# Turning the scan result of a decoder kernel with 32x32 block transposes on VectorE and sixteen small DMAs in place of eight TensorE transposes

## The chip, the cores and the metric

The kernel runs on one core of one Trainium2 chip. The metric is the device time of one execution in microseconds (us), lower is better. A core has TensorE (matrix products, results into PSUM; PE in the profile, its weight loads PEld), VectorE (DVE), ScalarE (ACT), GpSimd (POOL) and the queues that issue transfers; here almost all transfers are issued by SyncE (SP). The engines run their own instruction lists in order and meet at semaphores.

## The reference, cut to what matters

One decoder layer over 16 batches of 256 rows by 512 channels. The middle of its three parts is the one that the change touches: a decaying sum over the rows of the squared context, channel by channel (key and value are both the context), whose result multiplies the row x.

```python
def _L0_xattn_ref(q, k, v, decay):
    kv = kh * vh                      # k and v are both ctx
    def step(r, inc):
        r = d * r + inc               # a decay for each of 16 heads
        return (r, r)
    _, rs = jax.lax.scan(step, r0, kv_t)
    out = qh * jnp.moveaxis(rs, 0, 1)

x = _layernorm(x + attention(x))                       # 1
x = _layernorm(x + _L0_xattn_ref(x, ctx, ctx, decay))  # 2
x = _layernorm(x + ffn(x))                             # 3, a quantised FFN 512 -> 2048 -> 512
```

So the second sum is x * (1 + rs): each row of x times one plus its scan state.

## The kernel before

**Tiles.** A batch is 256 rows; row tiles put 128 rows on the partitions (two of them, q = 0 and 1, in `rows`), while the attention products and the scan put channels on the partitions (four tiles of 128 channels by 256 rows, `xT_in`, `ctx_sb`). The scan runs along the free dimension, so its result stands channels by rows in `ctx_sb` and has to be turned to rows by channels before it can meet `rows`.

**The software pipeline.** Each engine's list is written out by hand: a `lead`, then `body(j)` for j = 1 to 15 (called turn j here), then a `drain`. Turn j works on attention of batch j, on the projection, the first two layernorms and the first FFN product (`f`) of batch j-1, on the inner normalisation of the FFN of batch j-2, and on the second FFN product (`y`) and the last layernorm of batch j-3. What an engine does in a turn stands in one fixed order, so a wait at one place holds all that stands behind it on that engine.

**The path of the scan.** ScalarE squares the context in `ctx_sb` (`ctx_square`). VectorE, at the very end of its turn, runs four scans and one clip in place (`scan`, L1003 and L1006). In the next turn TensorE turns the result with eight 128x128 transposes into two PSUM banks (`r`, `r_product`, L1455), between `shiftT(j, 2)` and `shifted(j, 2)`. VectorE then forms x * (1 + state) in `layernorm2_sum` (L1029), once for each row tile, as one `scalar_tensor_tensor` whose first operand is the PSUM bank and whose second is `rows`:

```python
dv.scalar_tensor_tensor(rows_of(b)[:, q, :], bank_of("r", q, b), SCAN_SCALE, rows_of(b)[:, q, :],
                        ALU.add, ALU.mult).then_inc(S["ln2"], 1)
```

`statistics` follows each (L1013, L1015). After both, GpSimd makes the inverse deviation (`inverse_std2`), ScalarE normalises, VectorE quantises (`quantise_x`, which also fills `x_round`), ScalarE stores `xq`, SP turns it with a DMA transpose (`transpose_x`, xqT<-xq), and TensorE multiplies (`f`, L1467).

**What stands around it.** On VectorE the order in a turn is: `layernorm3_sum(j-3, 0)` (L1130), `layernorm1_sum(j-1, 0)`, `maxima(j, 1)` (L962), ..., `z_add(j-2, 0)` (L1085), `maxima(j, 2)`, `attn_norm`, `qk_lo(j, 3)`, `layernorm3_sum(j-3, 1)` (L1130), the two `layernorm2_sum(j-1, .)`, `z_max`, `maxima(j, 3)`, ..., `z_add(j-2, 1)`, `quantise_x(j-1)`, ..., `scan(j)`. On GpSimd, `attn_split(j, 1)` (L437, L440) is followed at once by `g_mul(j-2, 1)` (L547), a product of two SBUF tiles of 128x2048 elements. On TensorE, `y(j, 1)` (L1474) stands before `shiftT(j, 2)`; `shiftT(j, 3)` (L1367) waits for `maxima(j, 3)`, and all of the rest of TensorE's turn stands behind it. On SP a turn is `load_xT(j+1)`, `transpose_z(j-3, 1)` (hqT<-h, which `y(j, 1)` needs), `store_out`, `load_ctx(j)`, `transpose_x(j-1)`, `store_out`, `transpose_z(j-2, 0)`, `load_rows(j)`.

**PSUM banks.** Banks 6 and 7 go round between `y`, `o`, `r`, `v` and `f`; `take` makes the next user wait until the reader of the one before is done.

Of the kernel before, what the change touches and what calls it, by code (L numbers as in the profile page):

```python
# [12 lines left out]
ALU = mybir.AluOpType  # L13
AX_X = mybir.AxisListType.X

P = 128
# [27 lines left out]
NROW = NPART * NPART  # L44
NROWS = 3


def decoder_kernel(nc, x, xT, ctxT, W, L, bq, bk, bv, bo, decay, w1T, b1, ln_g, ln_b, w2T, b2, out):
    b1_scratch = nc.dram_tensor("b1_scratch", (NPART, INNER), BF16, kind="Internal").ap()

    with ExitStack() as ctx:
# [68 lines left out]
        def sem(name):  # L120
# [39 lines left out]
            (PE, "shifted_ready", 4), (PE, "scores_ready", 4), (PE, "qk_ready", 4), (PE, "v_ready", 2),  # L160
            (PE, "shiftT_ready", 4), (PE, "pv_ready", 4), (PE, "o_ready", 2), (PE, "rT_ready", 2),
            (PE, "f_ready", 8), (PE, "y_ready", 2),
# [7 lines left out]
            (DV, "qk_lo", 8), (DV, "max_done", 4), (DV, "shift_split", 8), (DV, "inverted", 12), (DV, "attn_done", 4),  # L170
            (DV, "scan_done", 5), (DV, "ln1", 6), (DV, "ln2", 6), (DV, "x_quant", 14),
            (DV, "z_added", 4), (DV, "z_quant", 12),
# [6 lines left out]
            (SP, "xT_loaded", 16), (SP, "x_loaded", 16), (SP, "ctx_loaded", 16), (SP, "out_stored", 32),  # L179
            (SP, "xqT_loaded", 16), (SP, "hqT_loaded", 64),  # L180
        ]
        per = {n: k for _, n, k in table}
# [19 lines left out]
        def half_rows(b, q):  # L202

            t = h_of(b, q)[:, :].bitcast(BF16)
            return t.rearrange("p (i k) -> p i k", i=2)[:, :, 0:INNER // 2]

        def rows_of(b):
            return rows[b % NROWS]

        users = [("y", 0, 3, "ln3", 1), ("o", 0, 1, "ln1", 1), ("o", 1, 1, "ln1", 4), ("y", 1, 3, "ln3", 4),  # L210
                 ("r", 0, 1, "ln2", 1), ("r", 1, 1, "ln2", 4), ("v", 0, -1, "v_stored", 1),
                 ("v", 1, -1, "v_stored", 2)]
        users += [("f", u, 1, "silu_done", u + 1) for u in range(8)]
# [3 lines left out]
        LAST, PRIOR, THIRD = NB - 1, NB - 2, NB - 3  # L217
        drain_bank = {("o", LAST, 0): 7, ("o", LAST, 1): 6, ("r", LAST, 0): 2, ("r", LAST, 1): 3,
                      ("y", THIRD, 0): 0, ("y", THIRD, 1): 1, ("y", PRIOR, 0): 4, ("y", PRIOR, 1): 5,
# [6 lines left out]
        def drain_hqT(b, q):  # L226

            if b == PRIOR and q == 0:
                return hqT[:, :, :]
            if b == LAST and q == 1:  # L230
                t = v_sb[PRIOR % 2][:, :, :].rearrange("p q d -> p (q d)").bitcast(BF16)
            else:
                t = probs[:, LAST - b if b == PRIOR else 0, :, :].rearrange("p i t -> p (i t)").bitcast(BF16)
            return t.rearrange("p (k t) -> p k t", t=P)

        def fz_of(b):
# [16 lines left out]
        def ffw(n):  # L253
            return h[FFW_BUFFER[n]][:, :]

        def flat(t):
            return t.rearrange("p a b -> p (a b)")

# [13 lines left out]
        def _(sp):  # L272
# [33 lines left out]
            def load_ctx(b):  # L306
                wait(sp, "rT_ready", b - 1, 2)
                if b == 0:
                    sp.wait_ge(u_merge, 5)
                sp.dma_start(ctx_sb[:, :, :], ctxT[b]).then_inc(S["ctx_loaded"], 16)  # L310

            def load_rows(b):
# [43 lines left out]
            def body(j):  # L356
                if alive(j, -1):
                    load_xT(j + 1)
                if alive(j, 3):
                    transpose_z(j - 3, 1)  # L360
                    store_out(j - 3, 0)
                load_ctx(j)
                transpose_x(j - 1)
                if alive(j, 3):
                    store_out(j - 3, 1)
                if alive(j, 2):
                    transpose_z(j - 2, 0)
                load_rows(j)
# [14 lines left out]

            def drain():
                transpose_z(THIRD, 1)
                transpose_x(LAST)
                store_out(THIRD, 0)
                store_out(THIRD, 1)
                transpose_z(PRIOR, 0)
                drain_transpose(PRIOR, 1)  # L390
                drain_transpose(LAST, 0)
                drain_transpose(LAST, 1)
                store_out(PRIOR, 0)
                store_out(PRIOR, 1)
                store_out(LAST, 0)
                store_out(LAST, 1)
# [546 lines left out]
        def _(dv):  # L943
# [53 lines left out]
            def scan(b):  # L997

                wait(dv, "ctx_squared", b, 1)
                if b == 0:  # L1000
                    dv.wait_ge(u_decay, 16 * GH)
                for c in range(KC):
                    dv.tensor_tensor_scan(ctx_sb[:, c, :], decay_col[:, c:c + 1].to_broadcast([P, T]),  # L1003
                                          ctx_sb[:, c, :], 0.0, ALU.mult, ALU.add).then_inc(S["scan_done"], 1)
                wait(dv, "scan_done", b, KC)
                dv.tensor_scalar(flat(ctx_sb[:, :, :]), flat(ctx_sb[:, :, :]), STATE_MAX, -STATE_MAX, ALU.min,  # L1006
                                 ALU.max).then_inc(S["scan_done"], 1)

            def statistics(ln, b, q, k, tile_rows):
# [15 lines left out]
            def layernorm2_sum(b, q):  # L1025

                wait(dv, "rT_ready", b, q + 1)
                wait(dv, "norm1", b, q + 1)
                dv.scalar_tensor_tensor(rows_of(b)[:, q, :], bank_of("r", q, b), SCAN_SCALE, rows_of(b)[:, q, :],  # L1029
                                        ALU.add, ALU.mult).then_inc(S["ln2"], 1)  # L1030
                statistics(2, b, q, 3 * q + 1, rows_of(b)[:, q, :])
# [281 lines left out]
        def _(pe):  # L1313
# [134 lines left out]

            def r(j, q):

                r_product(take(j, "r", q, "scan_done", j - 1, 5), q)

            def r_product(p, q):
                for kc in range(KC):
                    last = pe.transpose(p[:, kc * P:(kc + 1) * P], ctx_sb[:, kc, q * P:(q + 1) * P], ident[:, :])  # L1455
                last.then_inc(S["rT_ready"], 1)

            def f(j, u):
# [43 lines left out]
            def drain():  # L1502
# [3 lines left out]
                wait(pe, "probs_ready", LAST, 8)  # L1506
                wait(pe, "scan_done", LAST, 5)
                for q in range(NT):
                    r_product(bank_of("r", q, LAST), q)
                drain_y(THIRD, 0)  # L1510
# [7 lines left out]
                drain_f(5, "ln3", THIRD, 4)  # L1518
                drain_f(6, "ln2", LAST, 1)
                drain_f(7, "ln2", LAST, 4)  # L1520
                for at, (b, q) in enumerate(((PRIOR, 0), (PRIOR, 1), (LAST, 0), (LAST, 1))):
# [69 lines left out]
            def body(j):  # L1591
# [29 lines left out]
                if alive(j, 0):  # L1621
                    shiftT(j, 2)
                if alive(j, 1):
                    r(j, 0)
                    if j == 1:
                        pe.wait_ge(u_scale, 5)
                    r(j, 1)

                if alive(j, 0):
                    shifted(j, 2)  # L1630
# [11 lines left out]
                if alive(j, 0):  # L1642
                    shifted(j, 3)
                if alive(j, -1):
                    v(j, 1)
# [68 lines left out]
```

## Time and profile before

| | |
|---|---|
| median of 3 runs | 1051.52 us (1050.95 to 1052.96) |
| the profiled execution's own time | 1050.39 us |
| its span, first to last instruction | 1048.6 us |
| TensorE | 950.2 us busy, 91% of the span |
| VectorE | 891.9 us, 85% |
| ScalarE | 827.4 us, 79% |
| GpSimd | 605.4 us, 58% |
| the chain that ended last | 60% on TensorE, 26% on VectorE, 6% on transfers |
| mean granted TensorE clock | 0.962 of full speed |

A share of busy time is an average over lead, 15 turns and drain, and a TensorE that is shown busy is not one at its peak. What bounds a turn is read from the chain of waits within one turn and from the instructions that had to wait. Turns 3 to 14 repeat within a few tenths of a microsecond every 58 us; times below are from the span's start, and the rows shown of one turn are those of turn 7, from about 436 to 494 us.

### The profile page before, as it was taken

The page shows a single profiled execution, that of the slowest core. Times are in us where ns is not written, and L with a number is a line of the kernel's source. Part 1 is how long each engine was busy: PE and PEld are TensorE (multiplying, and loading weights), DVE is VectorE, ACT ScalarE, POOL GpSimd, SP SyncE. Part 2 cuts the span into 40 slices and gives each one's busy share as a digit, 9 for nine tenths or more (in the row PEclk, how much of TensorE's full clock was granted, in tenths as well). Part 3 has the DMA queues.
Part 4 walks back from the last instruction along what each step waited for, and adds up shares of the span by engine and source line. Part 5 has one row for each costly group of instructions (what it writes and reads, how often), then busy time and mean ns, then how long its engine had stood idle before and what let it go on. Part 6 is the DMA issues. An engine that isn't in the chain of part 4 may idle for free.

```text
span 1048.6 us, 23525 instructions
## 1 busy us (share of the span) xinstructions
PE 950.2 (91%) x9388; PEld 655.1 (62%) x9388; DVE 891.9 (85%) x1474; ACT 827.4 (79%) x957; POOL 605.4 (58%) x767
## 2 busy tenths in 40 slices
PE   5998997999999999999999999999999999978416
PEld 3766756676767767676767767676767677644102
DVE  4577868989898999989898989899898989995766
ACT  3646686888979797988888797978889797977684
POOL 2332337474766749485757658494757566572653
PEclk9999998999999999999999999999999999988668
DMA  9432200213122121323131121323231321122213
GB/s 357 158 111 113 72 3 21 74 52 84 23 71 61 43 76 52 84 52 83 35 100 23 56 68 44 83 52 84 52 84 21 79 56 54 42 52 63 53 30 91
DMA packets 106352, 73.68 MB, mean 70 GB/s; under 512 B 91386, under 2 KB 91386, under 8 KB 104451
## 3 DMA queue, kind: packets, MB, share of 16 engines
q1 hardware_dynamic: 105522, 70.34, 24.2%
q8 instruction: 75, 1.23, 0.5%
q10 hardware_dynamic: 720, 1.84, 0.5%
q14 instruction: 35, 0.28, 0.1%
HBM read 41.73 MB, written 8.40 MB: 48 GB/s over the span
## 4 chain that ended last, share of the span: by engine, by line
PE 60%; DVE 26%; DMA 6%; ACT 4%; issue 3%; POOL 1%; SPq 0%; POOLq 0%; DVEq 0%; ACTq 0%
PE bank L1333 21%; PE bank L1467 11%; PE bank L1474 9%; DMA xqT<-xq 5%; PE wave L1382 4%; PE bank L1396 4%; PE wave L1358 3%; DVE neg_max L962 3%; DVE h L1085 3%; PE bank L1400 3%; DVE stats L1013 3%; PE bank L1468 3%; DVE fz L1090 2%; DVE rows L1029 2%; DVE qx L1052 1%
## 5 line engine op out<-in xcount | busy, mean ns | idle before, releaser
L962 DVE TENSOR_REDUCE neg_max<-wave 128x8 f32<-128x2048 f32 x64 | 146.2, 2284 | 39.0 <-PE wave L1358 39.0
L547 POOL TENSOR_TENSOR h<-h,g_tile 128x2048 f32<-128x2048 f32 x30 | 139.9, 4663 | 39.1 <-ACT h L738 39.1
L655 ACT ACTIVATE probs<-wave 128x1024 f32<-128x1024 f32 x128 | 124.4, 1024 | 40.5 <-PE wave L1382 40.3
L1467 PE MATMUL bank<-w,xqT 128*128 128x512 fp8e4 x496 | 129.7, 384 | 20.6 <-DMA xqT<-xq 20.6
L437 POOL TENSOR_SCALAR attn_hi<-attn 128x256 fp32r<-128x256 f32 x64 | 31.8, 497 | 150.1 <-DVE attn L995 134.8
L717 ACT ACTIVATE h<-bank,qx 128x512 f32<-128x512 f32 x124 | 83.8, 689 | 24.4 <-PE bank L1468 22.1
L693 ACT ACTIVATE rows<-rows,rstd 128x512 f32<-128x512 f32 x96 | 74.3, 807 | 33.1 <-POOL rstd L453 18.5
L1085 DVE TENSOR_TENSOR h<-h,b_tile 128x2048 f32<-128x2048 f32 x32 | 84.0, 2624 | 17.0 <-POOL h L547 16.9
L1467 PEld LDWEIGHTS bank<-w,xqT 128*128 128x128 bf16 x496 | 47.8, 99 | 78.0 <-issue 17.4
L1474 PE MATMUL bank<-w,hqT 128*128 128x512 fp8e4 x416 | 94.3, 380 | 0.0
L496 POOL TENSOR_TENSOR rows<-rows,bo_tile 128x512 f32<-128x512 f32 x32 | 52.6, 1665 | 71.2 <-DMA rows<-x 71.2
L1003 DVE TENSOR_TENSOR_SCAN ctx_sb<-decay_col,ctx_sb 128x256 f32<-128x256 f32 x64 | 78.8, 1290 | 0.0
L1333 PE MATMUL bank<-xT_hi,wq_hi 128*128 128x256 f32 x256 | 78.4, 306 | 0.1
L440 POOL TENSOR_TENSOR attn_lo<-attn,attn_hi 128x256 fp32r<-128x256 f32 x64 | 73.7, 1151 | 5.3
L1382 PE MATMUL wave<-qk_parts 32*128 32x256 f32 x1536 | 73.4, 301 | 3.6 <-ACT shift_rows L677 3.6
L670 ACT ACTIVATE qk_parts<-bank,bias_qk 128x256 fp32r<-128x256 f32 x128 | 53.6, 474 | 25.9 <-PE bank L1333 25.9
L1396 PE MATMUL bank<-probs,v_sb 128*32 128x256 f32 x1024 | 70.6, 394 | 3.1 <-ACT probs L655 2.1
L1333 PE MATMUL bank<-xT_lo,wq_hi 128*128 128x256 f32 x256 | 73.3, 286 | 0.0
L1333 PE MATMUL bank<-xT_hi,wq_lo 128*128 128x256 f32 x256 | 73.2, 286 | 0.0
L738 ACT ACTIVATE h<-h,fs 128x2048 f32<-128x2048 f32 x32 | 66.8, 2089 | 7.8 <-POOL fs L538 7.8
L1358 PE MATMUL wave<-qk_parts 32*128 32x256 f32 x1536 | 63.7, 296 | 10.1 <-ACT probs L655 8.0
L1382 PEld LDWEIGHTS wave<-qk_parts 32*128 32x128 f32 x1536 | 56.9, 190 | 25.0 <-issue 20.1
(181 smaller groups left out, 2844.1 us busy)
## 6 DMA issues: line engine op xcount, KB each, us to landing
ctx_sb<-ctxT SPq DMA_DIRECT2D x16, 512.0 KB, 3.8
rows<-x SPq DMA_DIRECT2D x16, 512.0 KB, 4.0
out<-rows SPq DMA_DIRECT2D x32, 256.0 KB, 2.5
xT_in<-xT SPq DMA_DIRECT2D x15, 512.0 KB, 4.7
h<-w1T SPq DMA_DIRECT2D x4, 1024.0 KB, 14.6
h<-w2T SPq DMA_DIRECT2D x4, 1024.0 KB, 4.8
h<-Wq SPq DMA_DIRECT2D x1, 1024.0 KB, 6.2
h<-Wk SPq DMA_DIRECT2D x1, 1024.0 KB, 9.8
```

Of the source, the lines that this page charges most:

```text
L547: po.tensor_tensor(h_of(b, q)[:, :], h_of(b, q)[:, :], g_tile[:, :], ALU.mult).then_inc(done, 1)
L655: ac.activation(probs[:, kt, :, :], wave[:, :, kt * T:(kt + 1) * T], ACT.Exp, scale=SM_SCALE).then_inc(S["probs_ready"], 1)
L717: ac.activation(h_of(b, q)[:, n * FW:(n + 1) * FW], bank_of("f", u, b), ACT.Silu, scale=qx[:, X_DEQ, q:q + 1]).then_inc(S["silu_done"], 1)
L962: dv.tensor_reduce(neg_max[:, :, :], wave[:, :, :].rearrange("p j (t k) -> p j t k", t=NT), axis=AX_X, op=ALU.max, negate=True).then_inc(S ...
L1003: dv.tensor_tensor_scan(ctx_sb[:, c, :], decay_col[:, c:c + 1].to_broadcast([P, T]), ctx_sb[:, c, :], 0.0, ALU.mult, ALU.add).then_inc(S[" ...
L1085: dv.tensor_tensor(h_of(b, q)[:, :], h_of(b, q)[:, :], b_tile[:, :], ALU.add).then_inc(S["z_added"], 1)
L1333: last = pe.matmul(psum, lhsT, rhs, start=(first and i == 0), stop=(final and i == len(pairs) - 1))
L1358: last = pe.matmul(bank[head][:, qt * T:(qt + 1) * T], parts[at, qp, qt * P:(qt + 1) * P], parts[at, kp, :], start=(i == 0), stop=(i == 2))
L1382: last = pe.matmul(bank[head][:, kt * T:(kt + 1) * T], keys, queries, start=(i == 0), stop=(i == 3))
L1396: pe.matmul(bank[4][i * HD:(i + 1) * HD, 0:T], v_sb[b % 2][:, kt, ch:ch + HD], probs[:, kt, i, :], start=(kt == 0), stop=(kt == NT - 1))
L1467: pe.matmul(p[:, :], xqT[:, q, kc, :], w1[:, kc, n * FW:(n + 1) * FW], start=(kc == 0), stop=False)
L1474: last = pe.matmul(p[:, :], hqT[:, k, :], w2[:, k, :], start=(k == 0), stop=(k == FC - 1))
```

## The change

The state is no longer turned by TensorE. At the end of `scan`, VectorE writes the clipped state with two `transpose` instructions (each 128 partitions by 512 elements, every 32x32 block turned in itself) into `x_round`. SP then moves the blocks to their places with sixteen DMAs (`move_state`), each 32 partitions by 256 elements in pieces of 32 elements (128 bytes), from `x_round` back into `ctx_sb`, which now holds rows by channels. `layernorm2_sum` reads the state from `ctx_sb` in SBUF where it read a PSUM bank. `load_ctx` of the next batch waits for the second `layernorm2_sum`, where it waited for TensorE's transposes. The eight transposes are gone from TensorE's turn, from its drain and from the round of banks. SP's new `move_state(j-1)` stands right behind `load_xT(j+1)`, and first in SP's drain.

```diff
+SB = P // HD
...
-            (PE, "shiftT_ready", 4), (PE, "pv_ready", 4), (PE, "o_ready", 2), (PE, "rT_ready", 2),
+            (PE, "shiftT_ready", 4), (PE, "pv_ready", 4), (PE, "o_ready", 2),
...
-            (DV, "scan_done", 5), (DV, "ln1", 6), (DV, "ln2", 6), (DV, "x_quant", 14),
+            (DV, "scan_done", 7), (DV, "ln1", 6), (DV, "ln2", 6), (DV, "x_quant", 14),
...
+            (SP, "state_moved", 16 * SB * SB),
...
-                 ("r", 0, 1, "ln2", 1), ("r", 1, 1, "ln2", 4), ("v", 0, -1, "v_stored", 1),
-                 ("v", 1, -1, "v_stored", 2)]
+                 ("v", 0, -1, "v_stored", 1), ("v", 1, -1, "v_stored", 2)]
...
+        state_blocks = flat(x_round[:, :, :])
+        state_rows = flat(ctx_sb[:, :, :])
...
             def load_ctx(b):
-                wait(sp, "rT_ready", b - 1, 2)
+                wait(sp, "ln2", b - 1, 4)
...
+            def move_state(b):
+
+                wait(sp, "scan_done", b, 7)
+                for a in range(SB):
+                    for s in range(SB):
+                        to = state_rows[s * HD:(s + 1) * HD, :].rearrange("p (n a c) -> p n a c", a=SB, c=HD)
+                        block = state_blocks[a * HD:(a + 1) * HD, s * T:(s + 1) * T]
+                        sp.dma_start(to[:, :, a, :],
+                                     block.rearrange("p (n c) -> p n c", c=HD)).then_inc(S["state_moved"], 16)
...
                 if alive(j, -1):
                     load_xT(j + 1)
+                move_state(j - 1)
...
             def drain():
+                move_state(LAST)
                 transpose_z(THIRD, 1)
...
+                wait(dv, "scan_done", b, KC + 1)
+                wait(dv, "xq_stored", b - 1, 1)
+                blocks = state_blocks.rearrange("p (s q k c) -> p q k s c", s=SB, q=NT, c=HD)
+                for q in range(NT):
+                    dv.transpose(blocks[:, q, :, :, :],
+                                 ctx_sb[:, :, q * P:(q + 1) * P].rearrange("p k (s c) -> p k s c", c=HD)
+                                 ).then_inc(S["scan_done"], 1)
...
-                wait(dv, "rT_ready", b, q + 1)
+                wait(dv, "state_moved", b, 16 * SB * SB)
                 wait(dv, "norm1", b, q + 1)
-                dv.scalar_tensor_tensor(rows_of(b)[:, q, :], bank_of("r", q, b), SCAN_SCALE, rows_of(b)[:, q, :],
-                                        ALU.add, ALU.mult).then_inc(S["ln2"], 1)
+                dv.scalar_tensor_tensor(rows_of(b)[:, q, :], state_rows[:, q * D:(q + 1) * D], SCAN_SCALE,
+                                        rows_of(b)[:, q, :], ALU.add, ALU.mult).then_inc(S["ln2"], 1)
...
-            def r(j, q):
-
-                r_product(take(j, "r", q, "scan_done", j - 1, 5), q)
-
-            def r_product(p, q):
-                for kc in range(KC):
-                    last = pe.transpose(p[:, kc * P:(kc + 1) * P], ctx_sb[:, kc, q * P:(q + 1) * P], ident[:, :])
-                last.then_inc(S["rT_ready"], 1)
...
-                wait(pe, "scan_done", LAST, 5)
-                for q in range(NT):
-                    r_product(bank_of("r", q, LAST), q)
...
-                drain_f(6, "ln2", LAST, 1)
-                drain_f(7, "ln2", LAST, 4)
+                drain_f(6, "probs_ready", LAST, 8)
+                drain_f(7, "probs_ready", LAST, 8)
...
                 if alive(j, 0):
                     shiftT(j, 2)
-                if alive(j, 1):
-                    r(j, 0)
-                    if j == 1:
-                        pe.wait_ge(u_scale, 5)
-                    r(j, 1)
-
-                if alive(j, 0):
                     shifted(j, 2)
```

## Rows read from the trace of the kernel before

**Rows 1.** The chain of waits in turn 7: start, length (us), what.
```profile
458.59 3.57 PE bank L1474 x16
...
462.19 0.76 DVE rows L1130
...
480.97 3.38 DMA xqT<-xq
```

**Rows 2.** Timeline of TensorE, turn 7: start, length, instruction, [idle before, what ended it].
```profile
472.06 0.38 PE L1367 MATMUL wave<-ident,shift 128*128 128x128 f32 x2
...
484.49 1.02 PE L1467 MATMUL bank<-w,xqT 128*128 128x512 fp8e4 x4 [0.72 <-DMA xqT<-xq]
```

**Rows 3.** Timeline of VectorE, turn 7.
```profile
441.68 0.70 DVE L1006 TENSOR_SCALAR ctx_sb<-ctx_sb 128x1024 f32<-128x1024 f32 x1
...
446.65 2.29 DVE L962 TENSOR_REDUCE neg_max<-wave 128x8 f32<-128x2048 f32 x1 [1.14 <-PE wave L1358]
...
454.66 2.48 DVE L1085 TENSOR_TENSOR h<-h,b_tile 128x2048 f32<-128x2048 f32 x1 [1.34 <-POOL h L547]
...
463.81 0.68 DVE L1029 SCALAR_TENSOR_TENSOR rows<-bank,rows 128x512 f32<-128x512 f32 x1
...
465.35 0.68 DVE L1029 SCALAR_TENSOR_TENSOR rows<-bank,rows 128x512 f32<-128x512 f32 x1
```

**Rows 4.** Timeline of GpSimd, turn 7.
```profile
463.36 0.73 POOL L440 TENSOR_TENSOR attn_lo<-attn,attn_hi 128x256 fp32r<-128x256 f32 x1
464.05 4.66 POOL L547 TENSOR_TENSOR h<-h,g_tile 128x2048 f32<-128x2048 f32 x1
```

**Rows 5.** All instructions of two lines: ns shortest/median/longest, first and last start.
```profile
L1029 DVE SCALAR_TENSOR_TENSOR rows<-bank,rows x30: 678/679/682, 108.9 to 930.3; 128x512 f32<-128x512 f32 x30
...
L986 DVE STREAM_TRANSPOSE sums_T<-bank x64: 432/443/450, 46.6 to 946.9; 128x256 f32<-128x256 f32 x64
```

**Rows 6.** Timelines of VectorE and GpSimd, one place in the drain and one in turn 6.
```profile
987.92 6.49 DVE L1085 TENSOR_TENSOR h<-h,b_tile 128x2048 f32<-128x2048 f32 x1
...
987.45 4.80 POOL L547 TENSOR_TENSOR h<-h,g_tile 128x2048 f32<-128x2048 f32 x1 [4.84 <-ACT h L738]
...
434.16 1.99 DVE L1117 TENSOR_SCALAR h<-h,fz 128x2048 f32<-128x2048 f32 x1
...
433.80 3.48 POOL L496 TENSOR_TENSOR rows<-rows,bo_tile 128x512 f32<-128x512 f32 x2 [4.92 <-DMA rows<-x]
```

**Rows 7.** SP's timeline; DMA issues with KB and us to landing; the queue's packets, MB, share.
```profile
430.49 0.49 SPq L304 DMA_DIRECT2D xT_in<-xT  x1
452.59 2.62 SPq L334 DMA_TRANSPOSE hqT<-h  x2
...
2.14 0.83 SPq L279 DMA_DIRECT2D bv_col<-bv  x1
...
35.00 1.29 SPq L343 DMA_DIRECT2D b_scratch<-b_parts  x3
...
b_scratch<-b_parts SPq DMA_DIRECT2D x3, 4.0 KB, 2.4
...
hqT<-h SPq DMA_TRANSPOSE x58, 3.2
...
q1 hardware_dynamic: 105522, 70.34, 24.2%
```

**Rows 8.** Windows: length, busy time and instructions by engine, granted clock, DMA, GB/s.
```profile
930.00:937.30 7.30, 3.28 (x58) 1.94 (x58) 7.09 (x11) 5.22 (x7) 6.48 (x13) 1.00 0.29 94
937.30:950.90 13.60, 8.36 (x71) 4.36 (x72) 12.72 (x30) 10.44 (x11) 5.75 (x9) 0.50 0.23 53
...
90.80:94.20 3.40, 3.40 (x30) 1.66 (x23) 2.87 (x6) 2.90 (x6) 0.00 (x0) 0.50 0.62 255
```

**Rows 9.** The chain of waits at the transposes of turn 1 and of the drain.
```profile
107.97 1.70 PE bank L1455 x8
...
964.92 0.87 PE wave L1455 x8
```

More of the change, by code:

```diff
@@ L205, in half_rows, with flat @@
             return t.rearrange("p (i k) -> p i k", i=2)[:, :, 0:INNER // 2]
+        def flat(t):
+            return t.rearrange("p a b -> p (a b)")
         def rows_of(b):
@@ L217, in decoder_kernel @@
         LAST, PRIOR, THIRD = NB - 1, NB - 2, NB - 3
-        drain_bank = {("o", LAST, 0): 7, ("o", LAST, 1): 6, ("r", LAST, 0): 2, ("r", LAST, 1): 3,
+        drain_bank = {("o", LAST, 0): 7, ("o", LAST, 1): 6,
                       ("y", THIRD, 0): 0, ("y", THIRD, 1): 1, ("y", PRIOR, 0): 4, ("y", PRIOR, 1): 5,
@@ L254, in ffw @@
             return h[FFW_BUFFER[n]][:, :]
-        def flat(t):
-            return t.rearrange("p a b -> p (a b)")
         def merge_bank(m, kc):
@@ L1643, in body @@
                     shifted(j, 3)
+                if j == 1:
+                    pe.wait_ge(u_scale, 5)
                 if alive(j, -1):
```

## The prediction

> **What bounds the kernel now.** The page's chain first: it lies 60% on TensorE and 26% on VectorE (table above), so neither alone sets the time. Within one turn, the chain of waits shows how they share it [rows 1]: TensorE's y(j, 1) ends at 462.16; VectorE's layernorm3_sum starts at 462.19 and the chain stays on VectorE, gap after gap of some 0.02 us, through both layernorm2_sum and quantise_x to 480.9; the transpose xqT takes 3.38; then TensorE's f starts at 484.49. From there to the next y(j, 1) it is TensorE without a break. So a turn of 58 us is a TensorE stretch (f to y, some 36 us) and a VectorE stretch (18.8 us) with a transfer behind it. In the VectorE stretch TensorE has other work, and runs out of it 0.72 before f [rows 2]. In the TensorE stretch VectorE has spare time: it waits 1.14 for scores and 1.34 for GpSimd's g_mul [rows 3]. Work taken from TensorE pays only in its own stretch, and work put on VectorE costs in full only in its own.
>
> **Part by part.** The sum is made against the profiled execution, 1050.39 us.
>
> *The transposes leave TensorE.* Eight took 0.87 in the drain and 1.70 in turn 1, on the chain both times [rows 9]: -2.6 us. In the other turns they stand just behind y(j, 1), in the VectorE stretch, where TensorE waits for xqT at the end anyway [rows 2]: 0.
>
> *Two block transposes on VectorE.* A block transpose of 256 elements a partition takes 0.443 [rows 5]. For 512 I bound it by 0.44 (all overhead) and 0.89 (all length), and take 0.71, one element a cycle beyond a fixed part, like other 512-element VectorE rows here (0.68) [rows 3]: two make 1.45 with their gaps. They stand behind the clip that ends at 442.38. VectorE then reaches maxima(j, 1) at about 447.0 in place of 445.5, where it had waited until 446.65: 0.35 late, and z_add's wait of 1.34 swallows that [rows 3]. GpSimd's small deviation steps behind layernorm3_sum come 1.45 later too, and I leave 0.1 a turn for their way to g_mul (0 to 0.5 by the bounds).
>
> *Sixteen DMAs.* SP has nothing to issue between 431.0 and 452.59 [rows 7], so move_state starts at 443.9. One issue takes 0.43 in a row of three (1.29) and 0.83 at the dearest [rows 7]; the new ones have 256 pieces each, and I take 0.5, nearer to the run of three. Sixteen end at about 451.9; a small transfer lands 2.4 after its issue [rows 7]: state at 454, wanted at 463.81. Data: the queue's 105522 packets took 24.2% of 16 engines' span, 38 ns each [rows 7]; 4096 new ones at that price are 9.9 us of all sixteen engines, which still ends near 454, and these packets are smaller than the mean. Behind move_state on SP stands transpose_z(j-3, 1), now issued at 452.59: two issues, the second landing 3.2 later, about 457.1, for y(j, 1) at 458.59 [rows 1, 7]. So the transfers cost 0 so long as an issue stays under some 0.63; at 0.83 y would be 3.8 late. load_ctx moves about 5 us back and has until the end of the turn.
>
> *layernorm2_sum reads SBUF.* Here I see the price. With a PSUM operand L1029 takes 678 to 682 ns in all thirty rows [rows 5], though GpSimd's g_mul (L547, two SBUF inputs) runs beside it: L440 is busy from 463.36 to 464.09 and g_mul from 464.05 to 468.71, while the two L1029 stand at 463.81 and 465.35 and aren't touched [rows 3, 4]. Where both engines read two SBUF tensors they don't overlap: z_add in the drain took 6.49, starting 0.47 behind a g_mul of 4.80 [rows 6], against 2.48 in turn 7 [rows 3]; 4.33 of waiting and 2.16 of work, so VectorE stood until g_mul was through. Who goes first is seen in turn 6: GpSimd issued two L496 in a row, 433.80 to 437.28, and VectorE's L1117, issued at 434.16, ended at 436.15, in the middle of the pair [rows 6]. So the instruction already waiting goes before GpSimd's next.
>
> The Trainium skill says the same ("SBUF — State Buffer", Who interferes with whom): a VectorE instruction with two SBUF inputs contends with a GpSimd instruction that reads SBUF, as an exclusive lock, and the later one stands still until the other ends. The trace agrees, with the 6.49 above. L1029's own rows, which never moved, would price this edit at 0; the rule prices it at what is left of a g_mul.
>
> For turn 7: the first L1029 issues at 463.81, waits for L440 until 464.09, runs 0.6: 464.7, 0.2 late. g_mul goes next, about 464.65 to 469.3. The second L1029, wanted at 465.6, waits until 469.3 and ends at 469.9, against 466.03: 3.8 late, all of it in the VectorE stretch. Were g_mul to go first, the first L1029 would wait until 468.71: 4.8. Over the turns g_mul starts 0.19 to 0.27 behind the first L1029 in twelve (3 to 14) and 0.86 ahead of it in turn 15 (3.6 late there); in turn 2 VectorE then waits long for TensorE anyway; turn 1 has no g_mul. So 13 turns pay 3.8, with 4.8 as the upper bound.
>
> *What this does to TensorE.* shiftT(j, 3) waits for maxima(j, 3), and slides from 472.06 [rows 2] to 475.9; TensorE, rid of the transposes, runs dry about 471.7: some 4 us idle. In turn 15 it was busy for 3.28 of 7.30 us, and the granted clock then fell to 0.50 (1.2 GHz) for 13.6 us; in the lead it fell for 3.4 [rows 8]. A fall of 3.4 costs 1.7 of TensorE's work, of which 11.7 us lie between shiftT and f's place (484.49 less the 0.72): f at 475.9 + 11.7 + 1.7 = 489.3, against 488.3 for a late xqT alone. I take 0.7 a turn; bounds 0 (no fall) and 10.9 (all 11.7 at 1.2 GHz), and go by the shorter fall, since no second idle place of such length follows.
>
> **Sum.** 13 x (3.8 + 0.1 + 0.7) = 59.8; less 2.6: +57.2, so 1107.6 for the profiled execution, and 1108.7 from the median, which lies 1.1 above it. I say 1108.
>
> **The rivals.** *Not slower: the lock doesn't hold for this instruction.* scalar_tensor_tensor with an immediate might be let through where the plain sum of rows 6 wasn't. Then 13 x 0.1 - 2.6 = -1.3: 1049.1 for the profiled execution, 1050.2 from the median, 0.13% under before. It decides if a wait of the second L1029 stays under 0.2 us. Against it: both of its inputs come from SBUF, like z_add's.
>
> *The transfers are late.* If an issue costs 0.83, y(j, 1) is 3.8 late; its layernorm2_sum then meets a g_mul already running, so that the two delays overlap to about 4.8 a turn: 13 x (4.8 + 0.1 + 0.7) - 2.6 = +70, 1121. If the sixteen went one after the other at 2.4 us each, the state would land at 443.9 + 38.4 = 482.3, 18.5 late: 13 x 18.5 - 2.6 = +238, 1288. For it: sixteen small transfers in one queue. Against: three issues took 1.29 together and each landed after 2.4 [rows 7], so they overlap.
>
> The Trainium skill ("DMA: Bandwidth & Descriptors", Rules for kernel authors) wants small transfers coalesced, since under 64 KB one pays mostly overhead; these are 32 KB each. By its fixed 2 us each, in a row, I estimate a state 12 us late and a time near 1204; no row here shows transfers that wait for one another like that.
>
> *The block transposes are dear.* At three times their length (4.3 us) 2.8 us a turn would pass the slack of VectorE's TensorE stretch: +36 on top, 1144. The 0.443 of rows 5 hardly moves over 64 instances, so I give this little.
>
> **Chances.** Lock as worked out: 0.76, with a range of its own from 1087 (3.0 a turn in all) to 1131 (4.8, the 0.1 and 1.5 for the clock). Late transfers 0.10, of which 0.03 one after the other; half of the 0.10 above 1140. Not slower 0.10. Dear block transposes and the rest 0.04. The range 1080 to 1140 leaves out 0.18. About 0.2% (2.1 us) is what a measurement of this kernel tells from no change: slower 0.88, same 0.07 and faster 0.05, the last two from the second case, whose sum lies close to that bound.
>
> **What would show it.** Of the new profile: L1029's successor with one of its two instances at 4 us or more in turns 3 to 15, next to an L547 that ends just before it does (right), or at 0.7 (wrong); turns of 62 to 63 us; VectorE's transposes at 0.7; sixteen issues in some 8 us; state landing before VectorE asks for it; TensorE idle before shiftT(j, 3), and a granted clock under 1.00 in those turns, where it was 1.00 before. Wrong would be: VectorE waiting for state_moved, y waiting for hqT, or an L1029 that isn't held.

## The result, and the profile after

| | before | after |
|---|---|---|
| median | 1051.73 us (1050.95 to 1052.96, 4 runs) | 1123.58 us (1121.18 to 1125.73, 4 runs) |
| ratio | 1 | 1.0674 (95% interval 1.0652 to 1.0696) |
| profiled execution, its span | 1050.39, 1048.6 us | 1125.73, 1123.9 us |

Slower by 71 us (by the ratio), against the 57 forecast; 1123.6 lies within the range of 1080 to 1140. A kernel's time, below, is the median of its runs in the faster of the chip's two states. Below are the lines of the profile after that answer to those of before. First, the page's chain that ended last:

```profile
DVE 34%; PE 31%; SPq 15%; DMA 7%; issue 6%; ACT 5%; POOL 1%; ACTq 0%; POOLq 0%; DVEq 0%
SPq L323 13%; PE bank L1356 11%; DVE ctx_sb L1019 6%; DMA hqT<-h 5%; DVE rows L1052 5%; PE bank L1481 5%; PE bank L1488 4%; DVE neg_max L978 3%; PE wave L1405 3%; DVE stats L1036 3%; DVE h L1140 2%; DVE fz L1113 2%; SPq L348 2%; PE wave L1381 2%; PE bank L1419 2%
```

Where TensorE held 60% before, SP's issuing of the sixteen transfers (L323) now holds 13% by itself. Second, three groups of VectorE over the whole execution (count, busy us, mean ns, idle time before them and what ended it):

```profile
L1052 DVE SCALAR_TENSOR_TENSOR rows<-ctx_sb,rows 128x512 f32<-128x512 f32 x32 | 59.6, 1864 | 4.7 <-DMA ctx_sb<-x_round 4.7
L1028 DVE STREAM_TRANSPOSE x_round<-ctx_sb 128x512 f32<-128x512 f32 x32 | 20.9, 690 | 0.5
L1153 DVE SCALAR_TENSOR_TENSOR rows<-bank,fz,rows 128x512 f32<-128x512 f32 x28 | 20.4, 730 | 24.1 <-PE bank L1488 24.1
```

And layernorm3_sum in the kernel before:

```profile
L1130 DVE SCALAR_TENSOR_TENSOR rows<-bank,fz,rows 128x512 f32<-128x512 f32 x28 | 20.9, 747 | 2.0 <-PE bank L1474 1.2
```

layernorm2_sum (L1052) was L1029 with 679 ns in every instance [rows 5]; at 1864 it holds VectorE for 59.6 - 32 x 0.679 = 37.9 us more. And layernorm3_sum (L1153) waits 24.1 us for y, where it waited 1.2. The two make 61 us; the spans of the two profiled executions lie 75 us apart. The 4.7 us in front of L1052 are one wait, in the drain, for the state to land: behind the last layernorm2_sum of turn 15, the kernel after takes 2.5 us longer to its end. Third, the chain of waits in one turn (start, length, what), the successor of [rows 1], and GpSimd's timeline at the same place:

```profile
531.51 0.68 DVE x_round L1028
...
532.21 0.63 SPq L323
...
536.15 1.26 SPq L323
...
542.68 0.61 SPq L323
...
543.40 1.27 SPq L348
...
544.71 3.19 DMA hqT<-h
...
548.03 3.63 PE bank L1488 x16
...
551.68 0.76 DVE rows L1153
...
553.29 4.41 DVE rows L1052
...
558.55 0.69 DVE rows L1052
...
565.01 0.69 PE wave L1390 x2
```

```profile
551.84 0.73 POOL L456 TENSOR_TENSOR attn_lo<-attn,attn_hi 128x256 fp32r<-128x256 f32 x1
552.52 4.62 POOL L563 TENSOR_TENSOR h<-h,g_tile 128x2048 f32<-128x2048 f32 x1
```

The chain now runs through the change: the second block transpose ends at 532.2, SP issues sixteen transfers until 543.3, and only then hqT (L348), which y(j, 1) needs. y ends at 551.7, so late that g_mul (L563) starts 0.77 ahead of layernorm2_sum; the first L1052 stands until g_mul is through at 557.14 and ends at 557.7. In the kernel before, y came first and g_mul second. Over the turns this varies: the first L1052 took 2.6 to 5.1 us in 11 of the 13 turns from the third on, and 1.1 in two, where g_mul was nearly done. A turn takes 59 to 67 us, 63.6 in the mean, against 58.1. Last, windows of that turn (length, busy us of PE, PEld, DVE, ACT, POOL, granted clock, DMA, GB/s):

```profile
560.00:565.00 5.00, 0.97 (x5) 0.44 (x3) 4.93 (x6) 1.52 (x2) 4.00 (x12) 0.80 0.30 105
565.00:568.40 3.40, 3.38 (x12) 2.35 (x16) 3.30 (x7) 0.42 (x2) 2.08 (x5) 0.50 0.00 0
568.40:571.80 3.40, 3.40 (x40) 2.94 (x41) 3.23 (x7) 2.19 (x3) 2.08 (x2) 0.79 0.00 0
```

TensorE was busy for 0.97 of 5.00 us, and the granted clock fell to 0.50 (1.2 GHz). With 0.50 and 1.00 as its only levels, the means of the three rows make 2.0, 3.4 and 1.4 us at 0.50, 6.8 in all. Over the turns from 176 to 930 us it was 0.96, where it was 1.00 before.

So two things were to be told apart: the lock at layernorm2_sum, which the prediction made its main term, and sixteen issues in front of hqT, which it had put at 0.

### The profile page after: what moved, and what is told of

It is laid out like the page before. It is cut to its first block, busy times and chain, and to the rows that moved or that the text cites. A ratio compares the mean times of both kernels' runs of the same rounds, so it can differ in the third digit from the quotient of the medians.

```text
span 1123.9 us, 23542 instructions
## 1 busy us (share of the span) xinstructions
PE 961.0 (86%) x9260; PEld 655.7 (58%) x9260; DVE 943.9 (84%) x1506; ACT 829.0 (74%) x957; POOL 606.3 (54%) x767
## 3 DMA queue, kind: packets, MB, share of 16 engines
q10 hardware_dynamic: 720, 1.84, 0.5%
## 4 chain that ended last, share of the span: by engine, by line
DVE 34%; PE 31%; SPq 15%; DMA 7%; issue 6%; ACT 5%; POOL 1%; ACTq 0%; POOLq 0%; DVEq 0%
SPq L323 13%; PE bank L1356 11%; DVE ctx_sb L1019 6%; DMA hqT<-h 5%; DVE rows L1052 5%; PE bank L1481 5%; PE bank L1488 4%; DVE neg_max L978 3%; PE wave L1405 3%; DVE stats L1036 3%; DVE h L1140 2%; DVE fz L1113 2%; SPq L348 2%; PE wave L1381 2%; PE bank L1419 2%
## 5 line engine op out<-in xcount | busy, mean ns | idle before, releaser
L563 POOL TENSOR_TENSOR h<-h,g_tile 128x2048 f32<-128x2048 f32 x30 | 139.3, 4645 | 38.8 <-ACT h L754 38.8
L453 POOL TENSOR_SCALAR attn_hi<-attn 128x256 fp32r<-128x256 f32 x64 | 56.3, 879 | 170.1 <-DVE attn L1011 154.8
L1488 PE MATMUL bank<-w,hqT 128*128 128x512 fp8e4 x416 | 97.5, 389 | 19.1 <-DMA hqT<-h 19.1
L1405 PE MATMUL wave<-qk_parts 32*128 32x256 f32 x1536 | 80.9, 321 | 13.5 <-ACT shift_rows L693 13.5
L512 POOL TENSOR_TENSOR rows<-rows,bo_tile 128x512 f32<-128x512 f32 x32 | 48.0, 1522 | 81.4 <-DMA rows<-x 81.4
L1405 PEld LDWEIGHTS wave<-qk_parts 32*128 32x128 f32 x1536 | 63.2, 209 | 38.8 <-issue 20.6
L1488 PEld LDWEIGHTS bank<-w,hqT 128*128 128x128 bf16 x416 | 39.5, 99 | 72.3 <-issue 29.7
L995 DVE SCALAR_TENSOR_TENSOR qk_parts<-bank,bias_qk,qk_parts 128x256 fp32r<-128x256 f32 x128 | 55.6, 476 | 27.7 <-ACT qk_parts L686 27.7
L1019 DVE TENSOR_TENSOR_SCAN ctx_sb<-decay_col,ctx_sb 128x256 f32<-128x256 f32 x64 | 74.6, 1224 | 0.0
```

Of the source, the lines that this page charges most:

```text
L563: po.tensor_tensor(h_of(b, q)[:, :], h_of(b, q)[:, :], g_tile[:, :], ALU.mult).then_inc(done, 1)
L1405: last = pe.matmul(bank[head][:, kt * T:(kt + 1) * T], keys, queries, start=(i == 0), stop=(i == 3))
L1488: last = pe.matmul(p[:, :], hqT[:, k, :], w2[:, k, :], start=(k == 0), stop=(k == FC - 1))
```

## The experiments

My first theory for the profile after was that the late transfers set the turn and hide most of the lock; it came from one of the two turns in which layernorm2_sum waits only 0.4 us. The first four runs were made to test it against the prediction's lock.

**sbuf_read: the lock alone.** In the kernel before, only the operand:

```diff
-dv.scalar_tensor_tensor(rows_of(b)[:, q, :], bank_of("r", q, b), SCAN_SCALE, rows_of(b)[:, q, :],
+dv.scalar_tensor_tensor(rows_of(b)[:, q, :], flat(ctx_sb[:, :, :])[:, q * D:(q + 1) * D], SCAN_SCALE,
+                        rows_of(b)[:, q, :],
```

> The kernel before, in which layernorm2_sum takes its first operand from ctx_sb in SBUF as it stands, channels by rows and not turned (so its output is another one); TensorE's transposes still run and nobody reads them, and load_ctx waits for the second layernorm2_sum. No transfers and no block transposes are added. Theory 'lock' (the prediction's main term): the second layernorm2_sum waits some 3.8 us for g_mul in turns 3 to 15, with a lower clock behind it; 1095 to 1112 us. Rival 'late transfers alone' (the change's +72 us come from the sixteen issues, and the SBUF read costs nothing): layernorm2_sum keeps its 0.68 us in both instances; 1050 to 1053 us.

Measured: 1105.53 us, ratio 1.0497 (1.046 to 1.0533), +52 us. Its timelines of VectorE and GpSimd in one turn:

```profile
542.65 0.75 DVE L1130 SCALAR_TENSOR_TENSOR rows<-bank,fz,rows 128x512 f32<-128x512 f32 x1
...
544.26 0.82 DVE L1029 SCALAR_TENSOR_TENSOR rows<-ctx_sb,rows 128x512 f32<-128x512 f32 x1
...
545.95 4.18 DVE L1029 SCALAR_TENSOR_TENSOR rows<-ctx_sb,rows 128x512 f32<-128x512 f32 x1
```

```profile
544.49 5.09 POOL L547 TENSOR_TENSOR h<-h,g_tile 128x2048 f32<-128x2048 f32 x1
```

This is the prediction's turn: the first L1029 0.14 longer, g_mul next, the second L1029 held from 545.95 until 0.55 behind g_mul's end at 549.58. Counted from the start of layernorm3_sum, the second ends 3.64 us later than in the kernel before (7.48 for 3.84; predicted were 3.8). The same instruction with one operand moved from PSUM to SBUF, and no work added, goes from 0.68 to 4.18 us. The later start of load_ctx isn't the cause: no engine waits for that load in either trace. TensorE's idle place and the clock behind it are there too (windows of the same turn):

```profile
552.00:556.00 4.00, 0.77 (x4) 0.29 (x4) 3.93 (x5) 1.52 (x2) 3.25 (x12) 0.83 0.22 89
556.00:559.40 3.40, 3.40 (x12) 2.37 (x16) 3.30 (x7) 0.53 (x2) 2.14 (x4) 0.50 0.00 0
559.40:562.80 3.40, 3.40 (x39) 2.91 (x36) 3.23 (x8) 2.03 (x3) 1.97 (x2) 0.70 0.02 5
```

**gain_later, scan_early, both_moved: one cause taken away by another order.** In the kernel after:

```diff
+inverse_std2(j - 1)
 g_mul(j - 2, 1)
-inverse_std2(j - 1)
 x_rms(j - 1)
...
+scan(j)
 z_max(j - 2, 1)
 qk_lo(j + 1, 1)
 quantise_z(j - 2, 1)
-scan(j)
```

The upper half is gain_later (GpSimd), the lower scan_early (VectorE); both_moved has both.

> The kernel after, with GpSimd's inverse_std2(j-1) moved ahead of g_mul(j-2, 1), so that g_mul can't stand in front of either layernorm2_sum. The transfers stay as late as they were. Theory 'late transfers' (they set the turn, and the lock lies hidden behind them): the small remainder of the lock goes, 0.4 us in 13 turns, 1115 to 1121 us. Rival 'lock': the 3.8 to 4.6 us a turn come back, 1060 to 1075 us.

> The kernel after, with VectorE's scan(j) (with its clip and block transposes) moved ahead of z_max(j-2, 1), some 8 us earlier, so that the sixteen issues are over before SP has to issue hqT for y(j, 1). Theory 'late transfers over a hidden lock': y(j, 1) is no longer late, and the lock that it hid comes out at the second layernorm2_sum, 3.8 to 4.6 us in 13 turns less the 2.6 us of the transposes, 1095 to 1109 us. Rival 'late transfers alone': 1047 to 1052 us. Rival 'neither': 1120 to 1126 us.

> The kernel after with both moves: scan(j) ahead of z_max(j-2, 1), and inverse_std2(j-1) ahead of g_mul(j-2, 1). If late transfers and lock are the whole of the loss, either enough by itself for most of it: 1047 to 1052 us, with turns of 58 us. If something else that the change brought costs as well (the block transposes on VectorE, the packets of the transfers, the lost order of the PSUM banks), the time stays above 1056 us.

Measured: 1114.22 (1.0585, 1.0546 to 1.0624), 1113.12 (1.0575, 1.0536 to 1.0614) and 1093.23 us (1.0389, 1.037 to 1.0408). The first came out 0.8 us under the band of my theory, and for another reason: the lock had moved. The second lies in none of its three bands. The third stays above 1056 us, where it was expected if something else costs as well. This group is maxima's tiny sum of two SBUF tensors (128x8 elements), in gain_later and in the kernel after, both over the whole execution:

```profile
L986 DVE TENSOR_TENSOR shift<-neg_max,zeros 128x8 fp32r<-128x8 f32 x64 | 45.8, 716 | 2.2
```

```profile
L985 DVE TENSOR_TENSOR shift<-neg_max,zeros 128x8 fp32r<-128x8 f32 x64 | 15.3, 239 | 2.2
```

layernorm2_sum is down to 682 ns, but g_mul, now later, meets L986, which loses 45.8 - 15.3 = 30.5 us. In scan_early the new order has a price of its own: quantise_z(j-2, 1) now stands behind the scan, so the source of hqT is late whatever SP does (chain of waits, in front of y):

```profile
472.45 2.00 ACT h L724
474.45 0.02 issue
474.47 1.27 SPq L348
475.74 0.04 issue
475.78 4.86 DMA hqT<-h
```

both_moved has both of these prices (L986 at 709 ns). So none of the three is a clean test, and the next four change no order on VectorE or GpSimd, or say where they do.

**psum_read: the late transfers alone.** The kernel after, with a PSUM operand and TensorE's transposes again:

```diff
+    last = pe.transpose(p[:, kc * P:(kc + 1) * P], x_round[:, q, kc * P:(kc + 1) * P], ident[:, :])
...
     wait(dv, "state_moved", b, 16 * SB * SB)
-    dv.scalar_tensor_tensor(rows_of(b)[:, q, :], state_rows[:, q * D:(q + 1) * D], SCAN_SCALE,
+    dv.scalar_tensor_tensor(rows_of(b)[:, q, :], bank_of("r", q, b), SCAN_SCALE,
```

> The kernel after with the sixteen transfers and the block transposes kept, but with TensorE's eight transposes back (now of x_round, so the state used is another one and the output too), and layernorm2_sum reading their PSUM bank as in the kernel before; it still waits until the state has landed in ctx_sb, where nobody reads it. So the transfers are as late as in the kernel after, and no lock is possible at layernorm2_sum. Theory 'late transfers hide the lock': only the hidden remainder goes, 0.4 us a turn, less 2.6 us that the transposes bring back: 1115 to 1124 us. Rival 'the lock is the larger part': 1065 to 1080 us.

Measured: 1077.36 us, 1.0234 (1.0212 to 1.0257). This fells "late transfers hide the lock": without the lock 46 of the 71 us are gone, as the rival had it. It is also dearer than the prediction's 0 for the transfers. SP's timeline of one turn:

```profile
451.79 11.27 SPq L324 DMA_DIRECT2D ctx_sb<-x_round  x16
463.16 2.65 SPq L349 DMA_TRANSPOSE hqT<-h  x2
```

**split_moves: the kernel after, without the late hqT.**

```diff
-move_state(j - 1)
+move_state(j - 1, range(SB // 2))
 if alive(j, 3):
     transpose_z(j - 3, 1)
+move_state(j - 1, range(SB // 2, SB))
+if alive(j, 3):
     store_out(j - 3, 0)
```

> The kernel after, with SP issuing eight of the sixteen transfers before hqT (transpose_z(j-3, 1)) and eight behind it, and nothing else moved. hqT can then be issued when its source is ready, some 5 us before y(j, 1) wants it, and the state lands near the time at which layernorm2_sum asks. Theory 'late transfers hide the lock': y is on time and the lock comes out as in the kernel before with an SBUF operand (1105.5 us measured), less the 2.6 us of the transposes: 1096 to 1107 us, one of the two layernorm2_sum at some 4.2 us. Rival 'late transfers alone': 1048 to 1053 us. Rival 'the transfers cost by their data or their number, not by where SP issues them': 1118 to 1125 us.

Measured: 1116.03 us, 1.0598 (1.057 to 1.0625); its second layernorm2_sum takes 4.16 to 4.19 us in eleven turns, as in sbuf_read. With the lock in place, late transfers are worth only 0.76% or 8 us; the band of the theory was missed by 9 us, of which more below.

**psum_split: neither.** psum_read with the order of split_moves.

> As psum_read (layernorm2_sum reads a PSUM bank, TensorE's transposes are back and turn x_round, so the output is another one; 1077.4 us measured), with SP issuing eight of the sixteen transfers ahead of hqT and eight behind it. Theory 'the transfers cost by standing in front of hqT in SP's queue' (the issues took 0.61 us each and 0.05 between them in the traces, 10.5 us for sixteen, and one in a turn took over 1.1): y(j, 1) no longer waits for hqT, and what is left is the dead time of the block transposes, measured at 1.4 us: 1053 to 1058 us. Rival 'they cost by their packets or their number': 1072 to 1079 us. Between the two: the state lands late for layernorm2_sum instead.

Measured: 1054.78 us, 1.0021 (1.0008 to 1.0034). All sixteen transfers, both block transposes and all packets are in it, and 22.4 us (1.0234 less 1.0021) are gone by where SP issues eight of them. layernorm3_sum's wait for y, first in psum_read, then in psum_split:

```profile
L1155 DVE SCALAR_TENSOR_TENSOR rows<-bank,fz,rows 128x512 f32<-128x512 f32 x28 | 20.5, 731 | 27.1 <-PE bank L1499 27.1
```

```profile
L1157 DVE SCALAR_TENSOR_TENSOR rows<-bank,fz,rows 128x512 f32<-128x512 f32 x28 | 20.4, 730 | 0.6 <-PE bank L1501 0.2
```

**blocks_only: the block transposes alone**, as dead work at the end of scan in the kernel before:

```diff
+for q in range(NT):
+    dv.transpose(blocks[:, q, :, :, :],
+                 ctx_sb[:, :, q * P:(q + 1) * P].rearrange("p k (s c) -> p k s c", c=HD)
+                 ).then_inc(S["scan_done"], 1)
```

> The kernel before with the two block transposes of the kernel after added at the end of scan; they write x_round and nobody reads it before it is written anew, so they are dead work of 1.45 us a turn on VectorE. Theory of the prediction (VectorE's waits behind them swallow all but 0.1 us a turn): 1052 to 1055 us. Rival (what was left in the gated kernel, 0.9 us a turn, is theirs: they delay the next turn's layernorm3_sum, GpSimd's deviation behind it, and g_mul and z_add behind that): 1059 to 1066 us.

Measured: 1054.51 us, 1.0028 (1.0008 to 1.0048): 1 to 5 us, the prediction's 1.3 at the lower end. What paid for them is VectorE's wait for scores; the waits of before and of blocks_only over twelve to thirteen turns (total us, times, longest):

```profile
DVE neg_max L962 <- PE wave L1358: 17.4, 14, 4.0
```

```profile
DVE neg_max L966 <- PE wave L1369: 4.1, 2, 3.9
```

**split_gated: the change with both causes taken out.** split_moves, and GpSimd waits until VectorE is past:

```diff
 if alive(j, 2):
+    wait(po, "ln2", j - 1, 4)
     g_mul(j - 2, 1)
```

> As split_moves, and GpSimd's g_mul(j-2, 1) also waits until the second layernorm2_sum(j-1) is through; it then falls into the 5.3 us in which VectorE's next instructions (statistics, z_max, maxima) read one SBUF tensor or PSUM. If late transfers and lock are the whole of the loss, both are gone: 1047 to 1054 us, turns of 58 us, both layernorm2_sum at 0.7 us. If a further cost came with the change (block transposes, packets, clock), it stays: above 1058 us.

Measured: 1065.24 us, 1.0123 (1.0106 to 1.0139). In the turns both causes are gone, and 58 of the 71 us with them; the band was missed by 11 us. Of the 14.5 us between the two profiled spans, 4.0 lie behind turn 15's first layernorm2_sum and 0.9 in each of the twelve turns before it. In the drain all sixteen transfers still go ahead of hqT, and layernorm2_sum waits for the state:

```profile
L1055 DVE SCALAR_TENSOR_TENSOR rows<-ctx_sb,rows 128x512 f32<-128x512 f32 x32 | 24.7, 772 | 5.9 <-DMA ctx_sb<-x_round 5.9
```

In the turns the gate has a price: inverse_std2 stands behind g_mul, so ScalarE's second normalisation is late. That wait before and in split_gated:

```profile
ACT rows L693 <- POOL rstd L472: 6.0, 12, 0.6
```

```profile
ACT rows L712 <- POOL rstd L490: 36.5, 12, 3.1
```

ScalarE's shift_rows stands behind it, and TensorE's scores wait for that (before, then split_gated):

```profile
L1382 PE MATMUL wave<-qk_parts 32*128 32x256 f32 x1536 | 73.4, 301 | 3.6 <-ACT shift_rows L677 3.6
```

```profile
L1408 PE MATMUL wave<-qk_parts 32*128 32x256 f32 x1536 | 72.7, 299 | 36.1 <-ACT shift_rows L696 36.1
```

For xqT TensorE hardly waits any more (1.7 us over the turns, where it was 8.4), so the price runs through the scores and not through quantise_x. That it is the whole of the 0.9 a turn is argued; the block transposes are in this kernel too.

**swap_sums and swap_blocks: tries at a version that beats both kernels.** In both, layernorm2_sum goes ahead of y's reader; in the second the block transposes move too:

```diff
+layernorm2_sum(j - 1, 0)
+layernorm2_sum(j - 1, 1)
 layernorm3_sum(j - 3, 1)
-layernorm2_sum(j - 1, 0)
-layernorm2_sum(j - 1, 1)
...
 layernorm1_sum(j - 1, 0)
+turn_blocks(j - 1)        # swap_blocks: the two transposes, no longer in scan
```

> The kernel after, with SP issuing twelve transfers ahead of hqT and four behind it, and with VectorE's two layernorm2_sum(j-1) ahead of layernorm3_sum(j-3, 1), so that they no longer stand behind y(j, 1) and meet attn_split's short product (0.73 us) in place of g_mul. Theory 'lock at g_mul plus late transfers': both are nearly gone, what is left is a wait of some 0.4 us at L440 and the block transposes: 1049 to 1058 us if those cost 0.1 us a turn, 1058 to 1066 us if they cost 0.9. Rival 'the SBUF operand costs wherever it stands': above 1090 us.

> As swap_sums, with the block transposes moved from the end of scan into the next turn, behind layernorm1_sum(j-1, 0), where VectorE had 1.14 us of waiting for scores; eight transfers go ahead of hqT and eight behind it. If the block transposes cost by delaying layernorm3_sum(j-3, 0) and GpSimd behind it, that goes: 3 to 12 us faster than swap_sums, 1047 to 1054 us. If they cost nothing there, the same time as swap_sums.

Measured: 1069.72 (1.0172, 1.0154 to 1.0191) and 1100.80 us (1.046, 1.0415 to 1.0505). swap_sums has layernorm2_sum at 1113 ns over 176 to 930 us, so most of the lock is gone, yet it misses both of its bands; VectorE is then almost without a pause (its wait for scores is 4.8 us over 176 to 930, where it was 17.4). swap_blocks is a plain miss: the two transposes now start 3.1 us behind the end of the clip, the sixteen transfers come as much later, eight of them behind hqT where swap_sums has four, and layernorm2_sum waited for the state and then met g_mul (VectorE's timeline). The two kernels differ in more than the place of the transposes, so they don't price it.

```profile
478.17 0.69 DVE L1057 SCALAR_TENSOR_TENSOR rows<-ctx_sb,rows 128x512 f32<-128x512 f32 x1 [1.22 <-DMA ctx_sb<-x_round]
...
479.72 4.88 DVE L1057 SCALAR_TENSOR_TENSOR rows<-ctx_sb,rows 128x512 f32<-128x512 f32 x1
```

**before_zmax: is the VectorE stretch what bounds the kernel before?**

```diff
-z_max(j - 2, 0)           # behind layernorm2_sum(j - 1, 1)
...
 quantise_x(j - 1)
+z_max(j - 2, 0)
 quantise_z(j - 2, 0)
```

> The kernel before, with z_max(j-2, 0) (2.25 us on VectorE) moved from behind layernorm2_sum to behind quantise_x(j-1), and the waits' counts adapted; the change under study isn't in it. Theory of the prediction, that a turn is a VectorE stretch from y(j, 1) to xqT and a TensorE stretch from f to y(j, 1): the first becomes 2.25 us shorter, TensorE's wait of 0.72 us for xqT goes in some 13 turns, and the rest is TensorE's own work: 1040 to 1046 us. Rival 'VectorE's order there is slack': 1050 to 1053 us.

Measured: 1075.61 us, 1.0221 (1.0202 to 1.024): slower, outside of both bands. The first stretch got only 0.3 us shorter and not 2.25: maxima(j, 3) (L962) then waits for TensorE's scores (VectorE's timeline of one turn, moved and before):

```profile
472.87 0.75 DVE L1130 SCALAR_TENSOR_TENSOR rows<-bank,fz,rows 128x512 f32<-128x512 f32 x1 [0.19 <-PE bank L1473]
...
479.46 2.29 DVE L962 TENSOR_REDUCE neg_max<-wave 128x8 f32<-128x2048 f32 x1 [1.81 <-PE wave L1357]
```

```profile
469.06 2.28 DVE L962 TENSOR_REDUCE neg_max<-wave 128x8 f32<-128x2048 f32 x1
```

So L962 starts 6.59 us behind layernorm3_sum's start, where it was 6.87 [rows 1]. And z_max now stands ahead of quantise_z. ScalarE stores h (L708) ahead of the activation that frees f's banks (L717), and L708 waits for quantise_z. ScalarE's timeline, moved and before:

```profile
496.12 2.00 ACT L708 ACTIVATE h<-h,neg_round 128x2048 bf16<-128x2048 f32 x1 [2.83 <-DVE h L1117]
```

```profile
483.29 2.00 ACT L708 ACTIVATE h<-h,neg_round 128x2048 bf16<-128x2048 f32 x1 [0.41 <-DVE h L1117]
```

L708 had waited 0.41 us for quantise_z before and now waits 2.83; it starts 23.25 us behind layernorm3_sum's start, where it was 21.10. Behind it TensorE's f waits for L717, 16.3 us in 13 waits. So TensorE's scores are ready only 0.3 us before VectorE takes them, and a third stretch, from quantise_x through quantise_z to ScalarE and f's banks, stands right behind the VectorE stretch: moving z_max shortened the one by almost nothing and lengthened the other.

## Why the prediction was right and where it failed

**The number.** 1123.6 lies in the range, but not by the path that the forecast of 1108 was added up from: that had the transfers at 0. The range reached to 1140 also for the rival with late transfers (1121), and it is this rival that ran. So the hit is in part luck. Of the signs of being wrong that the prediction named, two are in the profile after: y waited for hqT (19.1 us in 13 waits), and VectorE waited for the state, once, in the drain. The held layernorm2_sum is there, but as the first of its pair and not as the second.

**The lock: right, and the larger cause.** The prediction had 3.8 us a turn at the second layernorm2_sum, 49 us over 13 turns. sbuf_read shows it alone: L1029 over the whole execution has a mean of 2152 ns over 32, which is 47 us above 679 ns each, and the time rose by 52. The rule of the Trainium skill ("SBUF — State Buffer", Who interferes with whom) that the later of the two stands still until the other ends agrees, with these 4.18 us. The first rival, that this instruction is let through, is out.

**The clock: right in kind, a longer fall, and a price that no run isolates.** Predicted was a fall of 3.4 us that costs 1.7 of TensorE's work. The three rows of sbuf_read make 1.4, 3.4 and 2.0 us at 0.50, 6.8 in all; in the last two TensorE is busy throughout, which costs 1.7 + 1.0 = 2.7. Of the turn, the prediction's own working gives 1.0 (489.3 less 488.3), and it took 0.7 without saying why. In the profiled execution of sbuf_read a turn takes 62.62 us for 58.10, so 4.52 more, of which 3.64 are the lock and 0.88 at most the clock's. That execution is the slowest of its four; against the +52 of the median, 5 us are left beside the lock's 47, or 0.4 a turn.

**The block transposes: right.** 690 ns each (0.71 predicted), and 1 to 5 us in all in the kernel before (1.3).

**The sixteen transfers: here the prediction failed.** The step that failed is the time of an issue on SP. It said that they cost 0 so long as an issue stays under 0.63 us, and took 0.5. The step from issue to issue is 0.61 and 0.04, and one of each sixteen took 1.0 to 1.84, so that sixteen took 10.8 to 11.9 us, 0.68 to 0.74 each. The bound was right (though at 0.83 its own rows make y 3.1 late and not 3.8) and the term mis-sized: alone (psum_read less psum_split) it is 22.4 us. This is the second rival, whose words fit the trace: y late, layernorm2_sum meeting a g_mul that already runs, the two delays overlapping. Its price was 1121, against 1123.6 measured, and 5.6 us a turn, against 5.5; its chance, 0.10, was too low: an issue was taken at the cheaper of two rows [rows 7] with no row for 256 pieces. Its worse case, that they go one after the other at 2.4 us, is out: the median landed 1.9 us after its issue while the next were issued, as the page gives it:

```profile
ctx_sb<-x_round SPq DMA_DIRECT2D x256, 32.0 KB, 1.9
```

The Trainium skill ("DMA: Bandwidth & Descriptors", Rules for kernel authors) advises to coalesce small transfers. No run here coalesced them; in psum_split the same sixteen cost 1 to 4 us, block transposes included, so the price lay in SP's queue and not in a fixed time of each transfer, and the 1204 that the prediction estimated from one is out.

The drain was left out of the prediction, but for 0.87 us of transposes that it gained. There the state isn't early: layernorm2_sum waits 4.7 us for it, and from turn 15's last one to the end the kernel takes 2.5 us longer.

**The two together.** Lock alone +52, late transfers alone +22 to 25, both +71. They overlap in a turn like the one shown: while y is late, g_mul runs off, and what is left of it decides the wait. Taken away last, the lock is worth 61 us (split_moves less psum_split) and the transfers 22; taken away first, 46 and 8.

**What stays open.** split_moves is 10.5 us above sbuf_read, though its hqT is issued in time and its block transposes and the transposes gone from TensorE should about cancel. In the two profiled executions it is 5.0 us, 4.0 of them ahead of turn 3, and a turn takes 62.8 us in one and 62.6 in the other; so little speaks for a cause within the turn. That the block transposes have used up VectorE's 1.3 us of waiting for scores, so that a lock is then paid in full, fits blocks_only and swap_sums, and is argued, not shown. The 2.6 us of TensorE's transposes were not measured by themselves. And the picture of two stretches is not complete: before_zmax shows a third one, which the sum did not need.

## What to carry to other kernels

When an operand moves from PSUM to SBUF, look for what GpSimd reads beside that instruction: here 0.68 us became 4.18, and moving GpSimd's instruction brought the same wait to a sum of 128x8 elements. Small transfers are paid in the queue that issues them: count issues times the measured step, name the transfer behind them, and first try to let that one go ahead, which here gave back 22 us with two lines where no lock stood behind them, and 8 where one did. Before a trace of 13 turns is explained, read the group's mean beside one turn, and test a cause by taking it away where no order changes.

## What the runs showed that was not expected

- An issue on SP of 32 partitions by eight pieces of 128 bytes took 0.60 to 0.63 us nearly always, and once in each sixteen 1.0 to 1.84; nothing in the trace says why.
- A VectorE instruction of 128x8 elements loses what is left of GpSimd's instruction as one of 128x512 does: in gain_later L986 took 2.52 us for 0.17, once a turn, and ended 0.03 behind a g_mul that had 2.49 to go.
